# The scan's B and C rows: from selection matmuls to a store in memory and one broadcast transfer per state

## The chip, the cores and the metric

The kernel runs on one core of a Trainium2 chip. The metric is the device time of one execution in microseconds (us). The kernel before has a median of 2842.82 us over three runs (2838.62 to 2860.75).

## What is computed

The input is eight sequences (b = 0 to 7) of 512 tokens with 128 features. Each passes through a layer norm, a Mamba block with what follows it (norms, a gated attention-like step, a small MLP), a mixture of experts in which a sequence picks 2 of 8, then causal attention with 16 heads of width 64, then a second mixture of experts in which each token picks 2 of 8. The change touches the Mamba block alone, whose core is the recurrence

```python
x_dbl = u @ x_proj_w.T
dt, Bm, C = jnp.split(x_dbl, [DT_RANK, DT_RANK + D_STATE], axis=-1)
delta = jax.nn.softplus(dt @ dt_proj_w.T + dt_proj_b)
def step(h, t):
    delta_t, B_t, C_t, u_t = t
    dA = jnp.exp(delta_t[..., None] * A)
    h = dA * h + delta_t[..., None] * B_t[:, None, :] * u_t[..., None]
    y = jnp.einsum('bdn,bn->bd', h, C_t)
    return (h, y)
```

There are 16 states n and 256 inner channels. Everything is float32.

## The kernel before

Features or inner channels lie on the 128 partitions and the 512 tokens along the row, so the 256 inner channels are two halves, 1024 values in a row. For one state n the recurrence over time is one scan instruction on VectorE. It takes three VectorE instructions in `front_step` (lines 1239 to 1262): D1 = DU x B (line 1245), the scan HS (line 1250), HC = HS x C (line 1262). ScalarE makes the decay factors DA (line 979), and GpSimd adds HC into Y (line 1601). B and C of one state are one row of 512 numbers each, the same for all 128 partitions, and they are needed on all of them. A selection matmul makes this: PE multiplies a 96 x 128 matrix of ones and zeros (`pick`, line 1140) by S3, which holds the 32 rows of B and C three times as bfloat16 parts that add up to float32, and leaves the row on all partitions of a PSUM bank (FB for B, line 635; FC for C, line 642). The three parts are made by six VectorE instructions, lines 1200 to 1209.

The work goes in laps, one for a sequence (`laps`, line 437). A lap has phase 1, in which the rest of the Mamba block and the first experts of sequence b are interleaved with the second experts of b-1 and the beginning of the Mamba block of b+1 (`front_start`), and phase 2, the attention of b with the 16 scan steps of b+1 laid between (f is b+1). The first sequence's Mamba block stands alone ahead of the first lap (`front`); its 16 scan steps follow each other with nothing else to do. The last lap has no scan.

Phase 2 is 64 tiles n, a tile being 128 query rows of one head; eight tiles are a pair of heads (j is the pair, i = n % 8 the place in it). The order of each engine is written out by hand:

- PE per tile: transposes of the probabilities (`turn`, line 832), the scores of tile n+3 (lines 821, 824), the product with the values of tile n-1 (line 844). At i = 0 and 2 it also projects q and k of the next pair (line 812). At i = 0 and 4 it makes B of a state, at i = 1 and 5 C.
- VectorE per tile: the row maximum of tile n+2 (line 1484), at i = 0 and 2 the rotated product for the next pair (line 1478), at i = 1 the division of the last pair (line 1496); then at i = 1, 2, 3 the parts D1, scan, HC of one state, and at i = 5, 6, 7 those of the next.
- ScalarE: the exponentials (line 1063), the copies of the transposes (line 1071), the bias for the rotation (line 1051).
- GpSimd: per rotation two additions or products (lines 1615 and 1618) at i = 0 and i = 2, and the addition into Y at i = 3 and i = 7.
- SyncE issues all transfers from one queue. In phase 2 these are the swaps of neighbouring rows for the rotation (`swap_pairs`, lines 505 to 513), two of 64 x 512 for each.

The scores use a ring of three PSUM banks, so PE can be at most about three tiles ahead of the exponentials, and these wait for the maxima.

## Time and profile before

| | |
|---|---|
| median of three runs | 2842.82 us |
| the profiled execution | 2849.43 us |
| its span, first to last instruction | 2847.6 us |
| PE busy | 2609.8 us, 92% |
| VectorE busy | 1804.3 us, 63% |
| ScalarE busy | 1235.0 us, 43% |
| GpSimd busy | 754.6 us, 27% |
| mean granted TensorE clock | 0.929 |

Busy shares are over the whole span. In the timeline a row is one instruction, or several of one kind in a row (x2, x4); instructions of one engine overlap a little, since the next one starts while the last drains. "Idle before" is how long the engine stood still ahead of a row, and behind the arrow stands what ended it. A clock of 1.00 is TensorE's full 2.4 GHz, 0.50 is 1.2 GHz.

### The profile page before, as it was taken

To read this page: it belongs to the slowest core of one execution; us is meant where nothing else is said; L and a number is where in the kernel's file an instruction comes from. 1 tells how busy PE (TensorE), PEld (TensorE's weight loads), DVE (VectorE), ACT (ScalarE), POOL (GpSimd) and SP (SyncE) were. 2 spreads that over 40 slices of the span, in tenths; PEclk is the share of its full clock that TensorE was granted. 3 is DMA by queue.
4 is the path that set the end of the run, shared out by engine and by line. 5 is a ranking of instruction groups with operands and counts; after the bars stand their busy time and mean duration, and the time that the engine had idled before them with its cause. 6 is when DMAs were issued, how large, how long until landed. Compare 5 with 4: busy or idle time off the path is not lost.

```text
span 2847.6 us, 35881 instructions
## 1 busy us (share of the span) xinstructions
PE 2609.8 (92%) x10560; PEld 1426.0 (50%) x10560; DVE 1804.3 (63%) x3214; ACT 1235.0 (43%) x2672; POOL 754.6 (27%) x429
## 2 busy tenths in 40 slices
PE   3267999999999999999999999999989999999999
PEld 1033555445554455545555455544555455545654
DVE  3953786567765677657866587557765587644334
...
DMA packets 28590, 61.76 MB, mean 22 GB/s; under 512 B 5464, under 2 KB 5856, under 8 KB 27744
## 3 DMA queue, kind: packets, MB, share of 16 engines
...
## 4 chain that ended last, share of the span: by engine, by line
PE 76%; issue 10%; DVE 8%; ACT 3%; POOL 2%; DMA 0%; SPq 0%; DVEq 0%; POOLq 0%; ACTq 0%
PE G L844 10%; PE G L821 9%; PE G L768 6%; PE G L769 6%; PE G L778 5%; PE G L832 5%; PE FM L821 5%; PE G L812 2%; PE G L861 2%; DVE HS L1250 2%; PE FM L748 2%; PE FM L596 2%; PE G L824 2%; PE G L568 2%; PE FM L812 1%
## 5 line engine op out<-in xcount | busy, mean ns | idle before, releaser
L1032 ACT ACTIVATE HS<-G 128x512 f32<-128x512 f32 x256 | 152.6, 596 | 608.4 <-PE G L769 607.1
L1601 POOL TENSOR_TENSOR Y<-Y,HC 128x1024 f32<-128x1024 f32 x128 | 301.1, 2352 | 351.3 <-DVE HC L1262 351.3
L844 PE MATMUL G<-REG 128*128 128x64 f32 x2560 | 383.4, 283 | 1.8
L1615 POOL TENSOR_TENSOR REG<-REG,cos_t 128x512 f32<-128x512 f32 x128 | 219.8, 1717 | 621.8 <-ACT REG L1051 621.8
L1413 DVE SCALAR_TENSOR_TENSOR HS<-HS,G 128x512 f32<-128x512 f32 x256 | 175.8, 687 | 298.7 <-ACT HS L1032 296.1
L844 PEld LDWEIGHTS G<-REG 128*128 128x128 f32 x2560 | 346.2, 201 | 11.0 <-ACT REG L1071 5.6
L1071 ACT ACTIVATE REG<-G 128x128 f32<-128x128 f32 (+3 forms) x512 | 222.2, 434 | 219.1 <-PE G L832 213.2
L1250 DVE TENSOR_TENSOR_SCAN HS<-DA,D 128x1024 f32<-128x1024 f32 x128 | 312.8, 2444 | 1.3
L821 PE MATMUL G<-REG 64*128 64x256 f32 (+3 forms) x688 | 289.8, 503 | 11.5 <-ACT REG L1063 11.3
L768 PE MATMUL G<-D,up_w 128*128 128x512 f32 x512 | 270.7, 611 | 7.8 <-DVE HC L1420 7.0
L778 PE MATMUL G<-HC,down_w 128*128 128x512 f32 x512 | 265.0, 602 | 3.9 <-DVE HC L1420 3.9
L769 PE MATMUL G<-D,gate_w 128*128 128x512 f32 x512 | 266.8, 603 | 0.0
L832 PE MATMUL G<-ident,REG 128*128 128x128 f32 x1280 | 237.7, 285 | 3.4 <-ACT REG L1071 2.9
L1578 POOL COPY XNB<-XN 128x512 f32<-128x512 f32 x8 | 4.9, 610 | 882.2 <-DVE REG L1389 867.5
L1484 DVE TENSOR_REDUCE maxes<-G 128x1 f32<-128x128 f32 (+3 forms) x344 | 164.1, 478 | 102.4 <-PE G L824 102.4
L1063 ACT ACTIVATE REG<-G,maxes 128x128 f32<-128x128 f32 (+3 forms) x344 | 179.5, 522 | 104.6 <-DVE maxes L1484 100.3
L979 ACT ACTIVATE DA<-DELTA,a_neg 128x511 f32<-128x511 f32 x256 | 180.2, 710 | 63.1 <-DVE HS L1250 62.9
L1420 DVE SCALAR_TENSOR_TENSOR HC<-HS,G 128x512 f32<-128x512 f32 x256 | 176.0, 688 | 25.6
L821 PEld LDWEIGHTS G<-REG 64*128 64x128 f32 x688 | 106.6, 194 | 156.8 <-issue 88.8
L1618 POOL TENSOR_TENSOR REG<-REG 128x512 f32<-128x512 f32 x128 | 168.0, 1312 | 58.7 <-DMA REG<-ROT 52.0
L832 PEld LDWEIGHTS G<-ident,REG 128*128 128x128 f32 x1280 | 172.1, 169 | 5.7 <-issue 4.8
L821 PE MATMUL FM<-REG 64*128 64x128 f32 (+3 forms) x336 | 145.4, 514 | 21.0 <-ACT REG L1043 18.9
...
## 6 DMA issues: line engine op xcount, KB each, us to landing
REG<-ROT SPq DMA_DIRECT2D x256, 128.0 KB, 2.0
EW<-experts SPq DMA_DIRECT2D x16, 514.5 KB, 4.1
...
```

The source lines that it names most:

```text
L768: pe.matmul(G[g][:, :], up_w[:, e, c * P:(c + 1) * P], XS[:, e % 2, :], start=True, stop=True)
L769: pe.matmul(G[g + 1][:, :], gate_w[:, e, c * P:(c + 1) * P], XS[:, e % 2, :], start=True, stop=True).then_inc(ug_mm.sem, 1)
L778: pe.matmul(G[4][:, :], down_w[:, n // CHUNKS, n % CHUNKS, :], HH[:, n % 4, :], start=n == 0, stop=n == T_STEPS - 1, skip_group_check=True ...
L821: pe.matmul(bank[:, 0:width], QK[lo:lo + DK, j % 2, 0, t * P:(t + 1) * P], QK[lo:lo + DK, j % 2, 1, 0:width], start=True, stop=False)
L832: mm = pe.transpose(G[2][:, c * P:(c + 1) * P], PR[:, n % 2, c * P:(c + 1) * P], ident[:, :])
L844: mm = pe.matmul(G[3][:, col:col + DK], PT[:, n % 2, c * P:(c + 1) * P], V[:, c, j * P + h * DK:j * P + (h + 1) * DK], start=c == 0, stop= ...
L979: act.activation(DA[:, n % 2, h, 1:S], DELTA[:, h, 1:S], ACT.Exp, scale=a_neg[:, h, n:n + 1]).then_inc(da_exp.sem, 1)
L1063: act.activation(PR[:, n % 2, 0:width], ring_bank[("score", n)][:, 0:width], ACT.Exp, bias=maxes[:, j % 2, i:i + 1], accum_out=rows[:, j % ...
L1071: act.activation(PT[:, n % 2, 0:width], G[2][:, 0:width], ACT.Copy).then_inc(pt_copy.sem, 1)
L1250: dve.tensor_tensor_scan(HS[:, :, :].rearrange("p h s -> p (h s)"), DA[:, n % 2, :, :].rearrange("p h s -> p (h s)"), D1[:, :, :].rearrang ...
L1601: pool.tensor_tensor(Y[:, :, :], Y[:, :, :], HC[:, n % 2, :, :], ALU.add).then_inc(y_add.sem, 1)
L1615: pool.tensor_tensor(ROT, ROT, cos_t[:, :], ALU.mult).then_inc(rope_d.sem, 1)
```

## The change

B and C of a sequence now come out of one float32 PSUM bank with 32 rows, are copied by one VectorE instruction to rows 32 to 63 of FT (BC), and are stored to a buffer in device memory (`bc_rows`, 32 x 512 float32, 64 KB). For each state one transfer reads its two rows and writes them to all 128 partitions (BCS, two buffers; 512 KB written per state). D1 and HC multiply by BCS, in SBUF, where they multiplied by FB and FC, in PSUM. The selection matmuls, the `pick` matrix, its source and the three-part split are gone. The load of state n waits for HC of state n-2.

```diff
-        row_of_sb = sb("row_of_sb", [96, 2 * STATES])
-        pick = sb("pick", [96, 2 * STATES, P], BF16)
-        S3 = sb("S3", [96, S], BF16)
-        S3B = sb("S3B", [96, S], BF16)
+        BCS = sb("BCS", [P, 2, 2, S])
-        R1, DT = FT[0:96, :], FT[0:RANK, :]
+        BC, DT = FT[32:32 + 2 * STATES, :], FT[0:RANK, :]
+        bc_rows = nc.dram_tensor("bc_rows", (2 * STATES, S), F32).ap()
...
+                if f is not None:
+                    store_bc(f)
+                    load_bc(f, 0)
+                    load_bc(f, 1)
                 if t is not None:
                     sp.wait_ge(out_d.sem, out_d.at(t))
                     sp.dma_start(outT[t], OUT).then_inc(out_st.sem, 16)
+
+            def store_bc(b):
...
+                sp.wait_ge(bc_copy.sem, bc_copy.at(b))
+                sp.sem_inc(sp_passed, 1)
+                sp.dma_start(bc_rows, BC).then_inc(bc_out.sem, 16)
+
+            def load_bc(b, n):
+
+                if n == 0:
+                    sp.wait_ge(bc_out.sem, bc_out.at(b))
+                    sp.sem_inc(sp_passed, 1)
+                if n >= 2:
+                    sp.wait_ge(hc_mul.sem, hc_mul.at(b, n - 1))
+                else:
+                    sp.wait_ge(hc_mul.sem, hc_mul.at(b - 1))
+                sp.sem_inc(sp_passed, 1)
+                sp.dma_start(BCS[:, n % 2, :, :], bc_rows.rearrange("(k n) s -> n k s", n=STATES)[n].partition_broadcast(P)).then_inc(bc_in[n % 2].sem, 16)
...
             def phase_2(b, f):
-                for m in range(2 * PAIRS):
-                    swap_pairs(b, m)
+                swap_pairs(b, 0)
+                swap_pairs(b, 1)
+                for n in range(N_TILES):
+                    j, i = n // PER_PAIR, n % PER_PAIR
+                    if i in PROJECT_AT and j + 1 < PAIRS:
+                        swap_pairs(b, 2 * (j + 1) + PROJECT_AT.index(i))
+                    if f is not None and i % 4 == 3 and n // 4 + 2 < STATES:
+                        load_bc(f, n // 4 + 2)
...
-                        mm = pe.matmul(out[0:96, :], w("x_bc", h * 96, 96), US[:, h, :], start=h == 0, stop=h == 1)
+                        mm = pe.matmul(out[0:2 * STATES, :], w("x_bc", h * 2 * STATES, 2 * STATES), US[:, h, :], start=h == 0, stop=h == 1)
...
-                pe.matmul(FB[:, :], pick[:, n, :], S3[:, :], start=True, stop=True).then_inc(b_mm.sem, 1)
...
-                pe.matmul(FC[:, :], pick[:, STATES + n, :], S3[:, :], start=True, stop=True).then_inc(c_mm.sem, 1)
...
-                    if f is not None and i % 4 == 0:
-                        front_b(f, 2 * j + i // 4)
-                    if f is not None and i % 4 == 1:
-                        front_c(f, 2 * j + i // 4)
...
-                    dve.tensor_copy(S3[:, :], out[0:96, :]).then_inc(bc_split.sem, 1)
...
-                    dve.tensor_copy(S3[64:96, :], R1[64:96, :]).then_inc(bc_split.sem, 1)
+                    dve.tensor_copy(BC, out[0:2 * STATES, :]).then_inc(bc_copy.sem, 1)
...
-                    dve.wait_ge(b_mm.sem, b_mm.at(b, n + 1))
+                    dve.wait_ge(bc_in[n % 2].sem, bc_in[n % 2].at(b, n // 2 + 1))
...
-                    dve.tensor_tensor(D1[:, :, :], DU[:, :, :], FB[:, :].unsqueeze(1).to_broadcast([P, HALVES, S]), ALU.mult).then_inc(db_mul.sem, 1)
+                    dve.tensor_tensor(D1[:, :, :], DU[:, :, :], BCS[:, n % 2, 0, :].unsqueeze(1).to_broadcast([P, HALVES, S]), ALU.mult).then_inc(db_mul.sem, 1)
...
-                    dve.tensor_tensor(HC[:, n % 2, :, :], HS[:, :, :], FC[:, :].unsqueeze(1).to_broadcast([P, HALVES, S]), ALU.mult).then_inc(hc_mul.sem, 1)
+                    dve.tensor_tensor(HC[:, n % 2, :, :], HS[:, :, :], BCS[:, n % 2, 1, :].unsqueeze(1).to_broadcast([P, HALVES, S]), ALU.mult).then_inc(hc_mul.sem, 1)
```

PE, phase 2, a stretch of the second pair of heads, tiles i = 0 to 2, in the kernel before (L812 projects q or k, L821 and L824 are a score, L832 the transposes, L844 the product with the values):

```order
L832 MATMUL G<-ident,REG 128x128
L635 MATMUL FB<-S,pick 128x512
L812 MATMUL G<-XN,W 128x512
L821 MATMUL G<-REG 128x512
L824 MATMUL G<-causal_bf,ident_bf 128x128
L844 MATMUL G<-REG 128x64 x4
L832 MATMUL G<-ident,REG 128x128 x2
L642 MATMUL FC<-S,pick 128x512
L821 MATMUL FM<-REG 128x128
```

and in the changed kernel, whose lines are 16 further down there:

```order
L848 MATMUL G<-ident,REG 128x128
L828 MATMUL G<-XN,W 128x512
L837 MATMUL G<-REG 128x512
L840 MATMUL G<-causal_bf,ident_bf 128x128
L860 MATMUL G<-REG 128x64 x4
L848 MATMUL G<-ident,REG 128x128 x2
L837 MATMUL FM<-REG 128x128
```

The two selection matmuls of a state are gone and the rest has kept its order.

VectorE, phase 2, from the division of a pair to the HC of its first state, in the kernel before, with what each waits for:

```order
L1496 TENSOR_TENSOR REG<-G,rows 128x512 [waits rec_d,pv_mm,ot_mm]
L1484 TENSOR_REDUCE maxes<-FM 128x1 [waits sc_mm]
L1245 TENSOR_TENSOR D<-DU,FB 128x1024 [waits b_mm]
L1484 TENSOR_REDUCE maxes<-G 128x1 [waits sc_mm]
L1478 SCALAR_TENSOR_TENSOR ROT<-G,V_,sin_t 128x512 [waits pj_mm,swap_in]
L1250 SCALAR_TENSOR_TENSOR HS<-DA,D 128x1024 [waits da_exp,db_mul]
L1484 TENSOR_REDUCE maxes<-FM 128x1 [waits sc_mm]
L1262 TENSOR_TENSOR HC<-HS,FC 128x1024 [waits y_add,c_mm,scan_d]
```

and in the changed kernel:

```order
L1493 TENSOR_TENSOR REG<-G,rows 128x512 [waits rec_d,pv_mm,ot_mm]
L1481 TENSOR_REDUCE maxes<-FM 128x1 [waits sc_mm]
L1243 TENSOR_TENSOR D<-DU,BCS 128x1024 [waits bc_in0]
L1481 TENSOR_REDUCE maxes<-G 128x1 [waits sc_mm]
L1475 SCALAR_TENSOR_TENSOR ROT<-G,V_,sin_t 128x512 [waits pj_mm,swap_in]
L1248 SCALAR_TENSOR_TENSOR HS<-DA,D 128x1024 [waits da_exp,db_mul]
L1481 TENSOR_REDUCE maxes<-FM 128x1 [waits sc_mm]
L1259 TENSOR_TENSOR HC<-HS,BCS 128x1024 [waits y_add,scan_d]
```

The order is the same. D1 waits for a transfer where it waited for a matmul, and D1 and HC read both inputs from SBUF where one came from a PSUM bank.

SyncE, phase 2, the swaps of one pair and the loads behind them, in the changed kernel; before, only the L538 rows stood here (as L513):

```order
L538 DMA REG<-ROT 64x512 [waits rope_d,rot_d]
L538 DMA REG<-ROT 64x512
L538 DMA REG<-ROT 64x512 [waits rope_d,rot_d]
L538 DMA REG<-ROT 64x512
L528 DMA BCS<-bc_rows 128x2x512 [waits hc_mul] x2
```

Two loads of 512 KB now stand between the second swap of a pair and the first of the next, in the same queue.

## Rows read from the trace of the kernel before

**Rows 1.** The page: busy time and share of the span, by engine

```profile
PE 2609.8 (92%) x10560; PEld 1426.0 (50%) x10560; DVE 1804.3 (63%) x3214; ACT 1235.0 (43%) x2672; POOL 754.6 (27%) x429
```

**Rows 2.** Busy time by stretch: a phase 1, then a phase 2

```profile
443.00:600.00 157.00, 156.11 (x509) 80.38 (x510) 92.04 (x222) 44.61 (x71) 6.04 (x5) 0.98 0.03 9
600.00:770.00 170.00, 162.56 (x812) 94.90 (x810) 129.29 (x178) 110.06 (x265) 89.55 (x50) 0.95 0.08 29
```

**Rows 3.** Timeline of PE: start, duration, tiles i = 0 and 1

```profile
661.74 0.38 PE L635 MATMUL FB<-S,pick 96*128 96x512 bf16 x1
661.96 1.02 PE L812 MATMUL FM<-XN,W 128*128 128x512 f32 x2
...
665.16 0.38 PE L642 MATMUL FC<-S,pick 96*128 96x512 bf16 x1
665.47 0.49 PE L821 MATMUL G<-REG 64*128 64x128 f32 x2
```

**Rows 4.** Timeline of VectorE over one pair of heads

```profile
660.64 1.21 DVE L1262 TENSOR_TENSOR HC<-HS,FC 128x1024 f32<-128x1024 f32 x1
...
663.02 0.75 DVE L1478 SCALAR_TENSOR_TENSOR ROT<-FM,V_,sin_t 128x512 f32<-128x512 f32 x1 [0.71 <-PE FM L812]
...
665.29 0.69 DVE L1496 TENSOR_TENSOR REG<-G,rows 128x512 f32<-128x512 f32 x1 [1.40 <-PE G L844]
...
666.49 1.21 DVE L1245 TENSOR_TENSOR D<-DU,FB 128x1024 f32<-128x1024 f32 x1
...
668.48 2.28 DVE L1250 TENSOR_TENSOR_SCAN HS<-DA,D 128x1024 f32<-128x1024 f32 x1
...
670.99 1.21 DVE L1262 TENSOR_TENSOR HC<-HS,FC 128x1024 f32<-128x1024 f32 x1
...
684.55 1.21 DVE L1245 TENSOR_TENSOR D<-DU,FB 128x1024 f32<-128x1024 f32 x1
```

**Rows 5.** Timeline of GpSimd over the same pair

```profile
661.93 2.35 POOL L1601 TENSOR_TENSOR Y<-Y,HC 128x1024 f32<-128x1024 f32 x1 [4.42 <-DVE HC L1262]
664.57 1.27 POOL L1615 TENSOR_TENSOR REG<-REG,cos_t 128x512 f32<-128x512 f32 x1 [0.30 <-ACT REG L1051]
666.53 1.27 POOL L1618 TENSOR_TENSOR REG<-REG 128x512 f32<-128x512 f32 x1 [0.69 <-DMA REG<-ROT]
669.37 2.46 POOL L1615 TENSOR_TENSOR REG<-REG,cos_t 128x512 f32<-128x512 f32 x1 [1.56 <-ACT REG L1051]
```

**Rows 6.** Timeline of the front's scan steps, VectorE and GpSimd

```profile
62.09 2.29 DVE L1250 TENSOR_TENSOR_SCAN HS<-DA,D 128x1024 f32<-128x1024 f32 x1
...
71.44 1.22 DVE L1245 TENSOR_TENSOR D<-DU,FB 128x1024 f32<-128x1024 f32 x1
...
71.67 2.34 POOL L1601 TENSOR_TENSOR Y<-Y,HC 128x1024 f32<-128x1024 f32 x1 [3.55 <-DVE HC L1262]
72.69 3.47 DVE L1250 TENSOR_TENSOR_SCAN HS<-DA,D 128x1024 f32<-128x1024 f32 x1
...
77.33 1.21 DVE L1245 TENSOR_TENSOR D<-DU,FB 128x1024 f32<-128x1024 f32 x1
```

**Rows 7.** Timeline, head of a phase 2: a GpSimd and a VectorE instruction

```profile
607.69 2.04 POOL L1618 TENSOR_TENSOR REG<-REG 128x512 f32<-128x512 f32 x1 [0.17 <-POOL REG L1615]
...
609.19 1.62 DVE L1232 TENSOR_TENSOR HS<-HS,D 128x1024 f32<-128x1024 f32 x1
```

**Rows 8.** Timeline of VectorE in the front: `pick`, and the copy behind the split

```profile
11.84 2.28 DVE L1140 CAST pick<-row_of_sb 96x4096 bf16<-96x4096 f32 x1
...
47.75 0.68 DVE L1213 COPY FT<-FM 8x512 f32<-8x512 f32 x1
```

**Rows 9.** DMA issues: count, KB each, us from issue to landing

```profile
REG<-ROT SPq DMA_DIRECT2D x256, 128.0 KB, 2.0
EW<-experts SPq DMA_DIRECT2D x16, 514.5 KB, 4.1
```

**Rows 10.** Busy time by stretch: one of four at this clock in that lap

```profile
972.00:982.00 10.00, 10.00 (x31) 5.96 (x31) 4.92 (x6) 3.34 (x10) 2.34 (x1) 0.50 0.00 0
```

More of the change, by code:

```diff
@@ L65 @@
 WEIGHTS = {}
-for _name, _n in (("in_res", INNER), ("x_bc", HALVES * 96), ("x_dt", HALVES * RANK),
+for _name, _n in (("in_res", INNER), ("x_bc", HALVES * 2 * STATES), ("x_dt", HALVES * RANK),
                   ("out_proj", HALVES * D), ("q", D), ("k", D), ("proj", D), ("fl", D), ("d1", HID),
@@ L227, in build @@
         dt_copy = signal("dt_copy")
-        bc_split = signal("bc_split", 6)
+        bc_copy = signal("bc_copy")
+        bc_out = signal("bc_out", 1, 16)
+        bc_in = [signal(f"bc_in{k}", STATES // 2, 16) for k in range(2)]
         dp_mm = signal("dp_mm", 2)
@@ L235, in build @@
         skip_y = signal("skip_y", 2)
-        b_mm, c_mm = signal("b_mm", STATES), signal("c_mm", STATES)
         da_exp = signal("da_exp", 2 * STATES)
@@ L337, in build @@
         by_pool = [du_d, skip_y, y_add, y_gate, xnb_d, rope_d]
-        by_sp = [x_in, xb_in, *ew_in, out_st, idx_rd, swap_in]
+        by_sp = [x_in, xb_in, *ew_in, out_st, idx_rd, swap_in, bc_out, *bc_in]
         F_STEPS, T_STEPS = 29, EXPERTS * CHUNKS
@@ L503, in phase_1 @@
                     sp.dma_start(outT[t], OUT).then_inc(out_st.sem, 16)
+            def store_bc(b):
+                for k in range(2):
+                    sp.wait_ge(bc_in[k].sem, bc_in[k].at(b - 1))
+                    sp.sem_inc(sp_passed, 1)
[10 more added lines that the diff above has]
+                    sp.wait_ge(hc_mul.sem, hc_mul.at(b - 1))
+                sp.sem_inc(sp_passed, 1)
+                sp.dma_start(BCS[:, n % 2, :, :], bc_rows.rearrange("(k n) s -> n k s", n=STATES)[n].partition_broadcast(P)).then_inc(bc_in[n % 2].sem, 16)
             def swap_pairs(b, m):
@@ L524, in front @@
                     sp.dma_start(dst, src).then_inc(s_late, 16)
+                store_bc(b)
+                for n in range(STATES):
+                    load_bc(b, n)
             laps(sp, front, phase_1, phase_2)
@@ L535, in _ @@
             pe.wait_ge(s_const, n_loads)
-            pe.wait_ge(s_made, 13)
+            pe.wait_ge(s_made, 12)
             def bank(key, b, f):
@@ L546, in bank @@
                     else:
-                        pe.wait_ge(hc_mul.sem, hc_mul.at(s))
+                        pe.wait_ge(relu_d.sem, relu_d.at(s))
                 else:
@@ L625, in front_delta @@
                 pe.matmul(FC[:, :], dt_lhs[:, P:INNER], DT, start=True, stop=True).then_inc(dp_mm.sem, 1)
-            def front_b(b, n):
-                if n:
-                    pe.wait_ge(db_mul.sem, db_mul.at(b, n))
-                else:
-                    pe.wait_ge(bc_split.sem, bc_split.at(b))
-                    pe.wait_ge(relu_d.sem, relu_d.at(b, 1))
-                pe.matmul(FB[:, :], pick[:, n, :], S3[:, :], start=True, stop=True).then_inc(b_mm.sem, 1)
-            def front_c(b, n):
-                if n:
-                    pe.wait_ge(hc_mul.sem, hc_mul.at(b, n))
-                else:
-                    pe.wait_ge(relu_d.sem, relu_d.at(b))
-                pe.matmul(FC[:, :], pick[:, STATES + n, :], S3[:, :], start=True, stop=True).then_inc(c_mm.sem, 1)
             def filter_step(b, p, f):
@@ L913, in front @@
                 front_delta(b, None)
-                for n in range(STATES):
-                    front_b(b, n)
-                    front_c(b, n)
             def late():
                 pe.wait_ge(s_late, n_late)
-                pe.wait_ge(s_made, 15)
+                pe.wait_ge(s_made, 14)
             laps(pe, front, phase_1, phase_2, late)
@@ L932, in _ @@
             act.activation(a_neg[:, :, :], a_neg[:, :, :], ACT.Exp).then_inc(s_alog, 1)
-            act.wait_ge(s_made, 13)
+            act.wait_ge(s_made, 12)
             def square(n, b):
@@ L943, in front_start @@
                     act.wait_ge(dp_mm.sem, dp_mm.at(f - 1))
+                    act.wait_ge(bc_out.sem, bc_out.at(f - 1))
                     square(n1, f)
@@ L1139, in _ @@
             dve.tensor_copy(causal_bf[:, :], causal_f).then_inc(s_made, 1)
-            dve.tensor_copy(pick[:, :, :], row_of_sb[:, :].unsqueeze(2).to_broadcast([96, 2 * STATES, P])).then_inc(s_made, 1)
             dve.tensor_copy(wg_cols[:, :], vec("w_g").to_broadcast([P, P])).then_inc(s_made, 1)
@@ L1560, in late @@
                 dve.tensor_scalar(q_b, q_b, DK ** -0.5, None, ALU.mult).then_inc(s_made, 1)
-                dve.wait_ge(s_made, 15)
+                dve.wait_ge(s_made, 14)
             laps(dve, front, phase_1, phase_2, late)
```

28 lines of the change are left out of this document (8 added, 20 removed).

## The prediction

> **What bounds the kernel now.** I read the page first. PE is busy 92% of the span, VectorE 63%, GpSimd 27% [rows 1]. The stretches say the same of both phases: PE 156.1 of 157 us in a phase 1, 162.6 of 170 in a phase 2 [rows 2]. So a matmul taken out is worth its time, if nothing else then comes last. VectorE is busy 129.3 of 170 us in phase 2 [rows 2], and there the change works, so I read one pair of heads engine by engine. The pair repeats every 684.55 - 666.49 = 18.06 us [rows 4]. In it VectorE waits for PE before the rotation (0.71 us) and before the division (1.40 us) [rows 4]: PE sets the pace, with VectorE a little behind. The front is different: there is no other work, VectorE never stops, and one scan step takes 77.33 - 71.44 = 5.89 us [rows 6].
>
> In the front a scan takes 3.47 us where the first took 2.29 [rows 6]. The first had no GpSimd work beside it; the later one starts at 72.69, inside the GpSimd addition that runs from 71.67 to 74.01, and ends at 76.16, 2.15 us after it. It did nothing until GpSimd was done. In phase 2 the reverse is seen: a GpSimd product of 1.27 us takes 2.46 when it is issued inside a scan (668.48 to 670.76) [rows 4, 5]. And a plain product of two SBUF operands, L1232, takes 1.62 us instead of about 1.22 when GpSimd runs until 609.73, 1.08 us before its end [rows 7]. The D1 product, which starts at 71.44 with one operand in PSUM, keeps its 1.22 us although GpSimd starts at 71.67, and GpSimd keeps its 2.34 [rows 6]. So on this chip a VectorE instruction with both inputs in SBUF and a GpSimd instruction exclude each other, and one with a PSUM input does not take part.
>
> The Trainium skill says this as a rule (SBUF — State Buffer, "Who interferes with whom"): a VectorE instruction with two SBUF inputs contends with a GpSimd instruction that reads SBUF, and the one that comes second blocks fully; one with at most one SBUF input does not. By that rule, the trace agrees, and the change puts 256 more instructions under the lock.
>
> **The change part by part.**
>
> *Selection matmuls, removed.* Start to start they take 661.96 - 661.74 = 0.22 and 665.47 - 665.16 = 0.31 us [rows 3], so 0.27. Phase 2 of seven laps has 7 x 32 = 224: 60 us of PE, 1.1 per pair. The 32 in the front lie under the scans and give nothing. This is the most that the laps can gain.
>
> *`pick` and the split.* `pick` takes 2.2 us ahead of the first matmul, which waits for it [rows 8]: -2.2. In the front the split holds the bank before the matmul of DT by one instruction of 0.7 us more than one copy does [rows 8]: -0.7. In the laps the split is VectorE work under a PE that is full (92.0 of 157 us busy) [rows 2]: 0, at most -0.7 a lap.
>
> *D1 and HC read SBUF twice.* Alone they should still take 1.21 us; the scan's and L1232's unblocked lengths give no reason for more. The cost is the exclusion.
>
> Front: GpSimd's addition becomes ready at 71.67, inside D1 (71.44 to 72.66) [rows 6]. It now waits about 1.0 us, the scan waits for it as today, and everything behind moves. Less the 0.14 us that a blocked instruction gains at the hand-over (2.15 against 2.29) it is 0.85; if nothing is gained and the whole D1 counts, 1.22. I take 1.0 for 15 steps: +15 (bounds +13 and +18; 0 if there is no exclusion).
>
> A pair in phase 2: the instructions that exclude each other are two each of D1, scan and HC, 2 x (1.21 + 2.28 + 1.21) = 9.40 us [rows 4], and on GpSimd two additions into Y and four of the rotation, 2 x 2.35 + 4 x 1.27 = 9.78 us [rows 5] (the 2.46 there is a 1.27 and its wait). Together 19.2 us, against a pair of 18.06. Ten hand-overs at 0.14 make it 17.8; between D1, scan and HC VectorE has a maximum of 0.2 to 0.3 us in which GpSimd sometimes has nothing, some 0.5: 18.3. Without gain at the hand-overs it is 19.7. So the shared access, which nobody waited long for, becomes as full as PE was. Going through the pair by hand, the places are: the second rotation's product and its sum stand in line behind the scan and HC, the addition into Y behind them, and so D1 or the scan of the second state (i = 5, 6) waits 1 to 2 us; the first D1 meets the rotation's sum (both start at about 666.5 [rows 4, 5]) and costs 0.5. Behind each of these on VectorE is the next row maximum, for which the exponential, the transposes and the next score wait. PE alone would want 18.06 - 1.1 = 17.0. The bounds are therefore 17.0 and 19.7. I take 18.7, nearer to 18.3 because the hand-over gain stands in two rows, and above it because PE, with a ring of three banks, will not take uneven maxima without loss. There are 7 x 7 pairs with rotations in them: 49 x 0.64 = +31 (bounds -54 and +80).
>
> The last pair of a lap has no rotations; its shared work is 14.1 us, but its last HC comes later by what the pair before left over: 0. The first has the routing of the tokens on VectorE beside it and PE already waits for VectorE there; D1 now also meets a rotation: +1 a lap, +7.
>
> *Transfers.* 128 loads of 512 KB. The nearest row is the expert transfer, 514.5 KB in 4.1 us [rows 9]. A load is issued behind HC of state n-2. In the front it has a whole step of 5.9 us or more; in a pair about half a pair, 9 us. So 4.1 us hides: 0. If a broadcast is slower, it costs what exceeds 5.9 in the front. The second load of a pair goes out about 1.2 us before the first swap of the next, in the same queue; the swap (2.0 us [rows 9]) would land at about 4.1 + 0.8 = 4.9 us after HC, and the rotation's sum will need it then. Also 0, with nothing to spare. The store of 64 KB lies in phase 1 or, in the front, beside softplus. On PE a matmul no longer waits for D1 or HC; it had not waited in phase 2.
>
> *Sum.* 2849.4 + 15 - 2.9 + 31 + 7 = 2899.5 for the profiled execution. That lies 6.6 above the median of the runs, so 2893.
>
> **The rivals.**
>
> A. *PE keeps the pace* (faster). VectorE is busy only 63% and waits 2.1 us in a pair [rows 1, 4]; if the exclusion falls into these waits, the 60 us come out in full. 2849.4 - 60 - 2.9 - 6.6 = 2780 without any cost in the front, 2795 with it. Against it: the shared work is longer than the pair that PE alone would want, 17.8 against 17.0.
>
> B. *Packed without loss.* The pair takes 18.06 as before, what PE gives is what the exclusion takes. Left are the front and the first pairs: 2849.4 + 12 + 7 - 6.6 = 2862.
>
> C. *The swap behind the load.* If a broadcast lands not after 4.1 but 5.6 us, as 128 copies of one 2 KB row might, each first swap is 1.5 us late, and with it the rotation's sum, the next rotated product on VectorE and the scan. 49 x 1.5 = +73: 2966. It decides from the point where load and swap together exceed 4.9 us. For it: one queue. Against: the setup's transfers, broadcasts among them, landed without delay.
>
> D. *The clock.* After gaps on PE the granted clock falls to 0.50 and a stretch of 10 us then does the work of 5; one lap has four of them [rows 10]. They begin in the first pair, where the change adds waiting. If each lap gets one such lap's 20 us: +100, 2990. Gaps of under 1 us within a pair, as I expect, do not look like those that made it fall.
>
> **How the numbers follow.** The forecast (a pair between 18.2 and 19.7) 0.57, A 0.13, B 0.20, C and D 0.10. Time 2893. The range takes in B, nearly all between it and A, and C: 2812 to 2975. The forecast's own range is 2872 to 2940. A change of under 1%, 28 us, is about what a measurement of this kernel cannot tell from none; that is 2814 to 2871. B is inside, a little of A's partial forms too. Faster 0.14, same 0.24, slower 0.62.
>
> **What would show it.** In the front a step of about 6.9 us instead of 5.89, with D1 at 1.22 and GpSimd's addition or the scan stretched. In a pair of phase 2, D1 and HC no longer all at 1.21 but many at 1.5 to 3 us, GpSimd's products too, VectorE's busy time up by some 100 us or more, and its waits for PE gone; in their place PE waits for the exponentials and these for the maxima. The pair at 18.7. PE's busy share below 92%. D1 never waits for the BCS transfer except perhaps at the very first. If D1 and HC stay at 1.21 everywhere with GpSimd beside them, the reading of the exclusion is wrong and A holds. If the rotation's sum waits for its swap longer than the 0.69 us in rows 5, C is at work. If the clock in the stretches falls below 0.95 in phase 2, D.

## The result and the profile after

The changed kernel takes 3001.36 us, the median of four runs (2989.34 to 3012.66), against 2851.78 us (2838.62 to 2870.98) for the kernel before: a ratio of 1.052, 95% interval 1.043 to 1.060. It is slower by some 5%. The sign was predicted; the size was not: 3001 lies outside the range of 2812 to 2975. The profiled execution took 2992.3 us, span 2990.5, at a mean granted clock of 0.879 where it was 0.929. Some executions of a kernel take over 1.5% longer than its fastest, at a lower granted clock: every ratio here leaves them out, the medians don't.

The page of the kernel after (busy time, clock by slice, the chain of waits, groups, DMA issues):

```profile
PE 2685.0 (90%) x10304; PEld 1477.5 (49%) x10304; DVE 1918.6 (64%) x3173; ACT 1223.3 (41%) x2672; POOL 839.0 (28%) x429
...
PEclk8567788999899899988889777997899978898999
...
PE 52%; issue 22%; POOL 12%; DVE 9%; ACT 2%; DMA 1%; POOLq 0%; SPq 0%; DVEq 0%; ACTq 0%
...
L1598 POOL TENSOR_TENSOR Y<-Y,HC 128x1024 f32<-128x1024 f32 x128 | 348.1, 2719 | 373.2 <-DVE HC L1259 373.2
...
L1248 DVE TENSOR_TENSOR_SCAN HS<-DA,D 128x1024 f32<-128x1024 f32 x128 | 375.1, 2930 | 1.3
...
L1073 ACT ACTIVATE REG<-G,maxes 128x128 f32<-128x128 f32 (+3 forms) x344 | 179.7, 522 | 153.2 <-DVE maxes L1481 152.3
L1615 POOL TENSOR_TENSOR REG<-REG 128x512 f32<-128x512 f32 x128 | 208.9, 1632 | 98.5 <-DMA REG<-ROT 90.4
...
L1243 DVE TENSOR_TENSOR D<-DU,BCS 128x1024 f32<-128x1024 f32 x128 | 194.3, 1518 | 2.6 <-POOL DU L1589 2.6
...
BCS<-bc_rows SPq DMA_DIRECT2D x128, 512.0 KB, 4.8
REG<-ROT SPq DMA_DIRECT2D x256, 128.0 KB, 2.1
```

and the groups of the kernel before that answer to four of them (before, the scan is L1250, the additions L1601 and L1618, the exponential L1063):

```profile
L1601 POOL TENSOR_TENSOR Y<-Y,HC 128x1024 f32<-128x1024 f32 x128 | 301.1, 2352 | 351.3 <-DVE HC L1262 351.3
...
L1250 DVE TENSOR_TENSOR_SCAN HS<-DA,D 128x1024 f32<-128x1024 f32 x128 | 312.8, 2444 | 1.3
...
L1063 ACT ACTIVATE REG<-G,maxes 128x128 f32<-128x128 f32 (+3 forms) x344 | 179.5, 522 | 104.6 <-DVE maxes L1484 100.3
...
L1618 POOL TENSOR_TENSOR REG<-REG 128x512 f32<-128x512 f32 x128 | 168.0, 1312 | 58.7 <-DMA REG<-ROT 52.0
```

PE has 256 matmuls of 512 columns less (10304 instead of 10560) and is nevertheless busy for 75 us more than in [rows 1]. Fewer instructions and more busy time means slower ones. VectorE grew by 114 us (the scan's mean from 2.44 to 2.93 us), GpSimd by 84: time that one spent shut out by the other. Two waits grew by half or more: the rotation's sum for its swap (52.0 to 90.4), and the exponential for the row maximum (100.3 to 152.3).

Where the time went can be summed from the timeline of VectorE, which divides once per pair of heads: 8 divisions and so 7 intervals ("pairs" below) in each of the seven laps with a scan. Each row below is one profiled execution; the columns hold sums over the seven laps, then how many of the 49 pairs are over 21 us, how often the granted clock falls to 0.50 within them, and how many of their microseconds are spent at 0.50 (where no fall is counted, these follow a fall ahead of the first division of a lap). The seventh pair of a lap has no rotations and is shorter (13.1 us before), so the sum is less than 49 usual pairs. The kernels of the experiments are in it already.

| kernel | first division at | 49 pairs | between the laps' pairs | usual pair | over 21 us | falls of the clock | us at 0.50 |
|---|---|---|---|---|---|---|---|
| before | 318.3 | 854.2 | 1454.2 | 18.06 | 1 | 0 | 23 |
| after | 329.2 | 979.0 | 1461.3 | about 19 | 14 | 19 | 260 |
| neither exclusion nor loads | 318.1 | 821.5 | 1428.7 | 17.47 | 0 | 0 | 11 |
| loads alone | 313.8 | 873.2 | 1432.7 | 18.0 | 3 | 4 | 76 |
| exclusion alone | 329.7 | 864.5 | 1467.2 | 18.18 | 1 | 0 | 36 |
| exclusion of HC alone | 318.0 | 829.0 | 1452.0 | 17.47 | 0 | 1 | 30 |
| exclusion of D1 alone | 333.0 | 845.0 | 1456.2 | 17.76 | 0 | 2 | 29 |
| loads behind swaps | 325.3 | 884.1 | 1455.8 | 18.55 | 0 | 5 | 49 |
| three buffers | 328.9 | 857.0 | 1455.5 | 18.18 | 0 | 1 | 20 |
| after, filled | 330.5 | 905.6 | 1466.8 | 19.1 | 1 | 0 | 18 |
| exclusion alone, filled | 331.3 | 881.2 | 1453.8 | 18.77 | 1 | 0 | 5 |
| B copied to PSUM | 315.2 | 823.7 | 1449.5 | 17.47 | 0 | 0 | 17 |
| B and C copied to PSUM (the second run) | 315.7 | 830.0 | 1439.0 | 17.64 | 0 | 0 | 14 |

Of the 142.9 us that the span grew, 10.9 lie ahead of the first division and 124.8 in the 49 pairs. In these the clock fell 19 times, and before the change never.

Ahead of it the front's step shows the exclusion as predicted. Timeline of VectorE and of GpSimd, kernel after:

```profile
61.39 1.22 DVE L1243 TENSOR_TENSOR D<-DU,BCS 128x1024 f32<-128x1024 f32 x1
62.64 4.31 DVE L1248 TENSOR_TENSOR_SCAN HS<-DA,D 128x1024 f32<-128x1024 f32 x1
66.98 1.22 DVE L1259 TENSOR_TENSOR HC<-HS,BCS 128x1024 f32<-128x1024 f32 x1
68.13 1.22 DVE L1243 TENSOR_TENSOR D<-DU,BCS 128x1024 f32<-128x1024 f32 x1
```

```profile
61.62 3.19 POOL L1598 TENSOR_TENSOR Y<-Y,HC 128x1024 f32<-128x1024 f32 x1 [5.06 <-DVE HC L1259]
```

GpSimd's addition starts inside D1 and now takes 3.19 us instead of 2.34 [rows 6]: it does nothing until D1 has ended, finishes at 64.81, and the scan, which was 3.47, is 4.31 and ends 2.14 us after it. The step is 68.13 - 61.39 = 6.74 us, 0.85 more than the 5.89 of [rows 6].

In a pair of phase 2 three engines are to be read together. Timeline of VectorE, GpSimd, SyncE and PE (only PE's rows with a wait), kernel after, lap 3. The SyncE rows are issues merged, and their length ends with the last issue, not with a landing:

```profile
1041.69 1.65 DVE L1243 TENSOR_TENSOR D<-DU,BCS 128x1024 f32<-128x1024 f32 x1
...
1044.25 0.75 DVE L1475 SCALAR_TENSOR_TENSOR ROT<-FM,V_,sin_t 128x512 f32<-128x512 f32 x1 [0.71 <-DMA REG<-ROT]
1044.92 2.71 DVE L1248 TENSOR_TENSOR_SCAN HS<-DA,D 128x1024 f32<-128x1024 f32 x1
...
1047.86 1.90 DVE L1259 TENSOR_TENSOR HC<-HS,BCS 128x1024 f32<-128x1024 f32 x1
...
1052.67 3.66 DVE L1248 TENSOR_TENSOR_SCAN HS<-DA,D 128x1024 f32<-128x1024 f32 x1
...
1056.57 1.21 DVE L1259 TENSOR_TENSOR HC<-HS,BCS 128x1024 f32<-128x1024 f32 x1
...
1060.88 1.64 DVE L1243 TENSOR_TENSOR D<-DU,BCS 128x1024 f32<-128x1024 f32 x1
```

```profile
1040.98 1.27 POOL L1612 TENSOR_TENSOR REG<-REG,cos_t 128x512 f32<-128x512 f32 x1
1044.20 1.27 POOL L1615 TENSOR_TENSOR REG<-REG 128x512 f32<-128x512 f32 x1 [1.95 <-DMA REG<-ROT]
1046.35 2.33 POOL L1612 TENSOR_TENSOR REG<-REG,cos_t 128x512 f32<-128x512 f32 x1 [0.88 <-ACT REG L1061]
1048.84 2.05 POOL L1615 TENSOR_TENSOR REG<-REG 128x512 f32<-128x512 f32 x1 [0.16 <-POOL REG L1612]
1050.85 3.34 POOL L1598 TENSOR_TENSOR Y<-Y,HC 128x1024 f32<-128x1024 f32 x1
```

```profile
1049.86 8.38 SPq L528 DMA_DIRECT2D BCS<-bc_rows  x2
1059.00 6.76 SPq L538 DMA_DIRECT2D REG<-ROT  x4
```

```profile
1041.32 0.41 PE L860 MATMUL G<-REG 128*128 128x64 f32 x2 [0.23 <-ACT REG L1081]
1044.08 0.66 PE L869 MATMUL G<-ident,REG 128*128 128x128 f32 x4 [0.37 <-ACT REG L1073]
1046.33 0.91 PE L837 MATMUL FM<-REG 64*128 64x384 f32 x2 [0.75 <-ACT REG L1061]
1048.59 1.12 PE L837 MATMUL G<-REG 64*128 64x512 f32 x2 [0.41 <-ACT REG L1073]
```

The pair is 1060.88 - 1041.69 = 19.19 us. The rotation's sum waits 1.95 us for its swap where it waited 0.69 [rows 5], and VectorE itself stands 0.71 us for that DMA. From D1's start to the scan's it is 3.23 us; before it was 668.48 - 666.49 = 1.99 [rows 4]. The last HC of the pair ends at 1057.78; the sum of the next pair waits until 1063.16, 5.4 us later (before: 4.7, from 661.85 to 666.53 [rows 4, 5]). PE, which was busy 162.6 of 170 us in a phase 2 [rows 2], waits in four small pieces of 0.23 to 0.75 us, 1.76 in all, for ScalarE, which waits for the maxima and for the rotation. In this pair the granted clock stays at 1.00.

### The profile page after: what moved, and what is told of

Its sections match the earlier page's. It is cut to its first block, busy times and chain, and to the rows that moved or that the text cites. A ratio compares the mean times of both kernels' runs of the same rounds, so it can differ in the third digit from the quotient of the medians.

```text
span 2990.5 us, 35609 instructions
## 1 busy us (share of the span) xinstructions
PE 2685.0 (90%) x10304; PEld 1477.5 (49%) x10304; DVE 1918.6 (64%) x3173; ACT 1223.3 (41%) x2672; POOL 839.0 (28%) x429
## 3 DMA queue, kind: packets, MB, share of 16 engines
q8 instruction: 97, 1.59, 0.2%
## 4 chain that ended last, share of the span: by engine, by line
PE 52%; issue 22%; POOL 12%; DVE 9%; ACT 2%; DMA 1%; POOLq 0%; SPq 0%; DVEq 0%; ACTq 0%
PE G L784 6%; PE G L785 6%; PE G L794 5%; PE G L860 5%; POOL REG L1615 4%; POOL REG L1612 4%; PE G L837 4%; DVE HS L1248 3%; POOL Y L1598 3%; PE FM L837 2%; PE G L848 2%; PE FM L764 2%; PE FM L630 2%; PE G L877 2%; PE G L602 2%
## 5 line engine op out<-in xcount | busy, mean ns | idle before, releaser
L1598 POOL TENSOR_TENSOR Y<-Y,HC 128x1024 f32<-128x1024 f32 x128 | 348.1, 2719 | 373.2 <-DVE HC L1259 373.2
L860 PE MATMUL G<-REG 128*128 128x64 f32 x2560 | 428.8, 306 | 9.4 <-ACT REG L1081 5.0
L860 PEld LDWEIGHTS G<-REG 128*128 128x128 f32 x2560 | 389.5, 223 | 20.5 <-issue 11.3
L1248 DVE TENSOR_TENSOR_SCAN HS<-DA,D 128x1024 f32<-128x1024 f32 x128 | 375.1, 2930 | 1.3
L837 PE MATMUL G<-REG 64*128 64x256 f32 (+3 forms) x688 | 320.6, 551 | 28.8 <-ACT REG L1073 14.8
L848 PE MATMUL G<-ident,REG 128*128 128x128 f32 x1280 | 262.5, 309 | 3.4 <-ACT REG L1081 2.7
L1073 ACT ACTIVATE REG<-G,maxes 128x128 f32<-128x128 f32 (+3 forms) x344 | 179.7, 522 | 153.2 <-DVE maxes L1481 152.3
L1615 POOL TENSOR_TENSOR REG<-REG 128x512 f32<-128x512 f32 x128 | 208.9, 1632 | 98.5 <-DMA REG<-ROT 90.4
L1243 DVE TENSOR_TENSOR D<-DU,BCS 128x1024 f32<-128x1024 f32 x128 | 194.3, 1518 | 2.6 <-POOL DU L1589 2.6
L848 PEld LDWEIGHTS G<-ident,REG 128*128 128x128 f32 x1280 | 192.2, 186 | 5.8 <-issue 3.8
L837 PE MATMUL FM<-REG 64*128 64x128 f32 (+3 forms) x336 | 163.2, 571 | 34.0 <-ACT REG L1053 19.6
## 6 DMA issues: line engine op xcount, KB each, us to landing
BCS<-bc_rows SPq DMA_DIRECT2D x128, 512.0 KB, 4.8
EW<-experts SPq DMA_DIRECT2D x16, 514.5 KB, 3.8
gate_w<-moe_gate SPq DMA_DIRECT2D x1, 2048.0 KB, 18.7
```

Of the source, the lines that this page charges most:

```text
L837: pe.matmul(bank[:, 0:width], QK[lo:lo + DK, j % 2, 0, t * P:(t + 1) * P], QK[lo:lo + DK, j % 2, 1, 0:width], start=True, stop=False)
L848: mm = pe.transpose(G[2][:, c * P:(c + 1) * P], PR[:, n % 2, c * P:(c + 1) * P], ident[:, :])
L860: mm = pe.matmul(G[3][:, col:col + DK], PT[:, n % 2, c * P:(c + 1) * P], V[:, c, j * P + h * DK:j * P + (h + 1) * DK], start=c == 0, stop= ...
L1243: dve.tensor_tensor(D1[:, :, :], DU[:, :, :], BCS[:, n % 2, 0, :].unsqueeze(1).to_broadcast([P, HALVES, S]), ALU.mult).then_inc(db_mul.sem, 1)
L1248: dve.tensor_tensor_scan(HS[:, :, :].rearrange("p h s -> p (h s)"), DA[:, n % 2, :, :].rearrange("p h s -> p (h s)"), D1[:, :, :].rearrang ...
L1598: pool.tensor_tensor(Y[:, :, :], Y[:, :, :], HC[:, n % 2, :, :], ALU.add).then_inc(y_add.sem, 1)
```

## The experiments

All edits are to the changed kernel unless another is named. Ratios are to the kernel before, run beside them, with 95% intervals. Where a kernel leaves work out, the text on record or the sentence ahead says so.

### The parts apart: neither, loads alone, exclusion alone

Without store and loads and the waits that belong to them, D1 and HC reading two PSUM banks that nothing writes for them (the result is then not the scan's):

```diff
-    store_bc(f)
-    load_bc(f, 0)
-    load_bc(f, 1)
...
-    dve.tensor_tensor(D1[:, :, :], DU[:, :, :], BCS[:, n % 2, 0, :]...
+    dve.tensor_tensor(D1[:, :, :], DU[:, :, :], FB[:, :]...
-    dve.tensor_tensor(HC[:, n % 2, :, :], HS[:, :, :], BCS[:, n % 2, 1, :]...
+    dve.tensor_tensor(HC[:, n % 2, :, :], HS[:, :, :], FC[:, :]...
```

> The changed kernel without its store and loads, and with D1 and HC reading the old PSUM banks FB and FC, which hold what the step before left there (no B or C is selected or loaded, so the scan computes with other numbers). It is what is left when the selection matmuls alone are taken out. All theories: PE sets the pace, a pair of heads takes 17.2 us against 18.06, and the time is about 60 us under the kernel before, 2785 to 2800, with the granted clock as before (0.93).

Measured: 2796.52 us, ratio 0.987 (0.983 to 0.991). The time is the expected one, the pair is not: 17.47 us instead of 17.2. The next keeps store and loads, whose data nobody reads, with D1 and HC on PSUM as above.

> As x1, but with the store and the 128 loads of 512 KB, whose data nobody reads (D1 and HC read the old PSUM banks). Theory T (the exclusion of VectorE and GpSimd makes the loss): within 10 us of x1. Theory Q (the swap of the rotation stands behind a load in the one queue, and what waits for it makes the loss): 30 us or more above x1, GpSimd's wait for the swap from 0.7 to 2 us a pair, pairs of 18 us or more.

Measured: 2842.57 us, ratio 0.999 (0.995 to 1.003), most pairs 17.9 to 18.2 and three over 21, as Theory Q had it. Its group of the rotation's sum:

```profile
L1615 POOL TENSOR_TENSOR REG<-REG 128x512 f32<-128x512 f32 x128 | 168.0, 1312 | 107.6 <-DMA REG<-ROT 98.0 <-POOL REG L1612 7.2 <-PE G L840 1.9
```

The sum itself is back at its 1312 ns, and the wait for the swap is 98.0 us, with no exclusion at all; without the loads it is 53.7. The loads make the swap late by themselves.

The third has D1 and HC on SBUF, as in the change, but no store and no loads; BCS holds a constant:

```diff
-    store_bc(f)
-    load_bc(f, 0)
-    load_bc(f, 1)
...
+    dve.memset(BCS[:, :, :, :], 0.01)
...
-    dve.wait_ge(bc_in[n % 2].sem, bc_in[n % 2].at(b, n // 2 + 1))
```

> The changed kernel without its store and loads: D1 and HC read both inputs from SBUF, BCS being filled once with a constant (B and C are not the computed ones). Theory T: most of the loss is here, 100 us or more above x1, D1, scan and HC stretched as in the changed kernel, and PE's gaps with a lower granted clock. Theory Q: within 30 us of x1. If the two act together, x3 lies between: a pair of 18.3 at full clock, 40 to 60 us above x1.

Measured: 2877.12 us, ratio 1.013 (1.007 to 1.020), pair 18.18. Timeline of VectorE, one pair:

```profile
1727.45 1.65 DVE L1233 TENSOR_TENSOR D<-DU,BCS 128x1024 f32<-128x1024 f32 x1
...
1729.88 2.49 DVE L1238 TENSOR_TENSOR_SCAN HS<-DA,D 128x1024 f32<-128x1024 f32 x1
...
1732.61 1.90 DVE L1249 TENSOR_TENSOR HC<-HS,BCS 128x1024 f32<-128x1024 f32 x1
```

The same blocked D1 and HC as in the full change, but the scan starts 2.43 us after D1 instead of 3.23. So of the 1.24 us by which that distance grew, the exclusion made 0.44 and the loads beside it 0.80. With the loads alone it is usually 2.1 us, hardly more than before: the late swap holds up the scan by that much only where the exclusion is there too. The time lies between the theories, but 81 us above x1 where 40 to 60 were expected.

What follows from the three: the removed matmuls and the split are worth 42 us (2838.77 against 2796.52), and by the medians the loads add 46 to that, the exclusion 81. The ratios are the better scale, since the changed kernel itself was measured at another time, beside other runs of the kernel before: 0.9991 - 0.9868 = 1.2 points for the loads and 1.0133 - 0.9868 = 2.65 for the exclusion, together a ratio of 1.026. The changed kernel is at 1.052. The 2.6 points between, some 74 us and well beyond the intervals, belong to neither alone.

### The loads moved: behind the swaps, and into a third buffer

```diff
-    if f is not None and i % 4 == 3 and n // 4 + 2 < STATES:
+    if f is not None and i == 3 and n // 4 + 2 < STATES:
         load_bc(f, n // 4 + 2)
+    if f is not None and i == 2 and j:
+        load_bc(f, 2 * j + 1)
```

> The changed kernel with the load of every second state issued behind the second swap of the next pair instead of ahead of the first. Nothing else changed. Theory T: within 20 us of the changed kernel. Theory Q: 50 us or more faster, the rotated product's wait for the swap gone.

Measured: 2891.56 us, ratio 1.020 (1.015 to 1.026), pair 18.55. The wait for the swap fell from 90.4 us to 34.0, but D1 now waits 50.7 us in total for its load, which it never did in the changed kernel. A wait was exchanged for a smaller one. The time is Theory Q's (3.1 points of ratio less than the changed kernel); the wait shrank and isn't gone.

With three buffers both loads of a pair can go out in the middle of it, ahead of any need. (Three counters that no engine waits for are also made one, here and in the versions that copy to PSUM.)

```diff
-    BCS = sb("BCS", [P, 2, 2, S])
+    BCS = sb("BCS", [P, 3, 2, S])
...
-    if f is not None and i % 4 == 3 and n // 4 + 2 < STATES:
-        load_bc(f, n // 4 + 2)
+    if f is not None and i == 3:
+        for k in (2 * j + 2, 2 * j + 3):
+            if 3 <= k < STATES:
+                load_bc(f, k)
```

> The changed kernel with three buffers for B and C instead of two and both loads of a pair issued in tile i = 3, so that no load is near a swap and each is issued a whole pair or half of one ahead of D1. If the queue is the whole difference between the changed kernel and the one without loads: 2865 to 2890, as x3 (2877), pairs of 18.2, no wait of D1 for BCS. If transfers cost something that is not their place in the queue: 2900 or more.

Measured: 2879.46 us, ratio 1.014 (1.007 to 1.022); usual pair 18.18, wait for the swap 38.4 us, no D1 waiting. That is the time, the pair and (38.5) the swap's wait of the exclusion alone, as the first of the two expectations has it, although all 128 loads of 512 KB are made, at 4.9 us each. The loads cost nothing by their bytes; what they cost is where they stand in the queue. Merely moving them takes 3.6% off the changed kernel.

### The clock: filler matmuls

One matmul of 512 bfloat16 columns per tile of phase 2, 448 in all, into a bank that nothing uses:

```diff
+    if f is not None:
+        if n == 0:
+            pe.wait_ge(relu_d.sem, relu_d.at(f))
+        pe.matmul(FB[:, :], ident_bf[:, :], FILL[:, :], start=True, stop=True)
```

> The changed kernel with one more bfloat16 matmul of 512 columns behind the transposes of every tile of phase 2 while there is a scan; its result is not read. 448 matmuls of some 0.22 us are 99 us more work for PE, 1.8 us a pair. Theory C (the gaps that exclusion and queue leave on PE make the clock fall, and the pairs at half clock are half of the loss): the fillers stand in PE's gaps, the granted clock rises from 0.88 to 0.92 or more, pairs of 22 to 27 us become rare, and the time is not above that of the changed kernel and may be 50 us under it. Theory N (the clock is no cause; PE's waits for maxima are): the time rises by 30 to 99 us and the clock stays.

Measured: 2919.17 us, ratio 1.027 (1.019 to 1.035): PE has more to do and the kernel is 82 us faster than the changed one by the medians, some 70 by the ratios (1.052 against 1.027). Stretches of phase 2 in lap 2, first the kernel after and then the filled one (busy time of PE, PEld, DVE, ACT, POOL; then the granted clock, DMA share, GB/s):

```profile
700.00:710.00 10.00, 8.19 (x35) 4.48 (x34) 8.15 (x9) 5.61 (x15) 6.57 (x5) 0.81 0.30 88
710.00:720.00 10.00, 10.00 (x48) 5.65 (x47) 7.81 (x8) 5.34 (x15) 3.81 (x2) 0.85 0.27 62
...
740.00:750.00 10.00, 8.65 (x41) 5.22 (x40) 9.27 (x9) 5.96 (x15) 7.20 (x5) 0.85 0.25 89
750.00:760.00 10.00, 10.00 (x44) 5.47 (x42) 7.51 (x8) 5.11 (x15) 3.52 (x2) 0.80 0.22 65
```

```profile
700.00:710.00 10.00, 9.99 (x57) 6.22 (x57) 8.34 (x10) 5.82 (x16) 5.34 (x3) 1.00 0.34 99
710.00:720.00 10.00, 9.70 (x54) 5.55 (x52) 8.94 (x11) 6.32 (x18) 7.98 (x4) 1.00 0.26 73
...
740.00:750.00 10.00, 9.99 (x55) 5.90 (x55) 8.38 (x12) 5.91 (x15) 4.49 (x4) 1.00 0.27 80
750.00:760.00 10.00, 9.81 (x60) 6.05 (x57) 9.29 (x8) 6.16 (x16) 8.09 (x4) 1.00 0.24 79
```

Read the first fence in pairs of rows: a stretch in which PE has gaps (8.19 and 8.65 of 10 us busy), in or behind which the granted clock leaves 1.00, and then one in which PE is busy throughout and yet does only 48 or 44 matmuls, where the filled kernel, fillers included, does 54 to 60. Some of the time PE runs there at the lower of its two levels, 1.2 instead of 2.4 GHz. With the fillers the clock is 1.00 in all these rows, it doesn't fall once within the 49 pairs, and of the 14 pairs over 21 us one is left. That is Theory C. The waits that make the gaps are still there: the rotation's sum still waits 90.2 us for its swap.

What PE did ahead of the fall in 740:750, kernel after (only its rows with a wait; the granted clock is 1.00 until 747 and 0.54 in the microsecond behind it):

```profile
739.48 0.41 PE L860 MATMUL G<-REG 128*128 128x64 f32 x2 [0.23 <-ACT REG L1081]
742.23 0.66 PE L869 MATMUL FM<-ident,REG 128*128 128x128 f32 x4 [0.37 <-ACT REG L1073]
744.30 0.91 PE L837 MATMUL G<-REG 64*128 64x384 f32 x2 [0.58 <-ACT REG L1061]
746.56 1.59 PE L837 MATMUL G<-REG 64*128 64x512 f32 x2 [0.41 <-ACT REG L1073]
```

Four waits, 1.59 us in all, and none is longer than 0.58. Shortly ahead of each of the 19 falls PE had waited at least twice; in 13 of them no single wait was over 0.88 us, in the other six one was 1.0 to 2.3. But the pair of lap 3 above has the same four waits with 1.76 us in all, and its clock stays at 1.00. What decides between the two is not shown.

The trace gives the clock's price without the fillers too. In the kernel after, lap 3 has 6.8 us at half clock in its seven pairs and they take 128.4 us; lap 5 has 62.0, and they take 149.9. That is 21.5 us for 55.2 at half clock, 0.39 each. The 49 pairs have 260 - 23 = 237 us more at half clock than before: an estimate of 92 us.

To see whether fillers gain anywhere, the same were put into the version with the exclusion alone.

> The control for the filled version of the changed kernel: the same 448 filler matmuls (their result is never used) in the version without loads, where D1 and HC read a constant from SBUF and so compute wrong numbers at the right cost. Without fillers this version took 2877.12 us with pairs of 18.18 us and hardly any of 22 to 27 us. Theory (the fillers gain only by keeping the clock up where the loads had let it fall): there is little to win here and up to 99 us of TensorE's work to pay, part of it inside its gaps; 2865 to 2925 us, not below 2865. Rival (fillers gain in any version, by some other way than the gaps that the loads make): the same gain as in the changed kernel, about 80 us, so 2795 to 2830 us.

Measured: 2895.96 us, ratio 1.017 (1.013 to 1.022), pair 18.77 instead of 18.18. Here they cost: 0.59 us a pair, 16.7 us in the 49 pairs, and 19 us by the medians (0.4 points by the ratios, whose intervals overlap). The gain of 80 us that the rival wanted is excluded. So of these two versions the fillers gain in the one whose clock falls. The two filled versions also give what the loads cost when the clock stays up: 905.6 - 881.2 = 24 us in the 49 pairs.

### The exclusion: D1 or HC

The version with the exclusion alone, with D1 on PSUM and so HC's exclusion only:

```diff
-    dve.tensor_tensor(D1[:, :, :], DU[:, :, :], BCS[:, n % 2, 0, :]...
+    dve.tensor_tensor(D1[:, :, :], DU[:, :, :], FB[:, :]...
```

> As x3 (no loads, a constant in BCS), but D1 reads the old PSUM bank FB, so only HC and the scan read both inputs from SBUF. Half of the exclusion. In the front the step should be 5.9 us as in the kernel before, since only D1 met the addition there. In a pair HC still meets the rotation, and the first and second D1 no longer hold up anything: between x1 (2796) and x3 (2877), nearer to x1, 2805 to 2840, a pair of 17.5 to 17.9.

Measured: 2818.29 us, ratio 0.993 (0.990 to 0.996); pair 17.47, front step 5.9, both as with no exclusion; the ratio is 0.6 points higher than there, with intervals that just overlap. In the other, HC reads FC in PSUM and D1 reads BCS. (The text on record has the two letters exchanged: D1 reads B from SBUF, and HC reads its C from a bank that nothing writes.)

> This kernel is the changed one without its loads (BCS holds a constant), with D1's exclusion alone: D1 reads C from SBUF, and HC reads B from a PSUM tile that nothing writes; both products are wrong numbers at the right cost. Theory (all of the exclusion's price is D1, HC's costs nothing): the pair is 18.2 us, as with both, the time 2860 to 2885 us, and the time of a half-tile step in the opening stage 6.74 us. Rival (the two share the price, and HC's came for free only where D1's was gone): the pair is 17.7 to 18.0 us and the time 2835 to 2860 us.

Measured: 2835.04 us, ratio 0.998 (0.994 to 1.003); pair 17.76, front step 6.74. This was the rival's pair, and the time stands at the edge of its range. Alone, HC's exclusion costs no pair time, and D1's 0.29 us; together they cost 0.71. In the front D1 makes all of it, since it is D1 that delays GpSimd's addition. In a pair HC is blocked just as long without D1's exclusion, but nothing comes of it. One pair with HC's exclusion alone, VectorE and GpSimd:

```profile
1706.19 1.91 DVE L1249 TENSOR_TENSOR HC<-HS,BCS 128x1024 f32<-128x1024 f32 x1
...
1709.09 1.20 DVE L1233 TENSOR_TENSOR D<-DU,FB 128x1024 f32<-128x1024 f32 x1
...
1711.01 2.68 DVE L1238 TENSOR_TENSOR_SCAN HS<-DA,D 128x1024 f32<-128x1024 f32 x1
```

```profile
1709.19 2.36 POOL L1588 TENSOR_TENSOR Y<-Y,HC 128x1024 f32<-128x1024 f32 x1
```

and the same scan and addition of a pair with both exclusions:

```profile
1737.42 3.66 DVE L1238 TENSOR_TENSOR_SCAN HS<-DA,D 128x1024 f32<-128x1024 f32 x1
```

```profile
1735.60 3.33 POOL L1588 TENSOR_TENSOR Y<-Y,HC 128x1024 f32<-128x1024 f32 x1
```

HC takes 1.91 us alone and 1.90 with both. What differs comes behind it: GpSimd's addition starts beside the second D1. With D1 on PSUM it runs at once (2.36 us) and the scan behind takes 2.68; with D1 on SBUF it has to wait for D1 (3.33), and the scan for it (3.66). It is the meeting of the two that costs.

By the ratios HC's share on top of D1's is 1.5 points, 43 us, give or take some 22 by the two intervals. The two profiled executions differ by 2885.2 - 2857.8 = 27.4 us, of which 19.5 are in the pairs (864.5 - 845.0) and 11.0 between the laps' pairs. So no stage hides the rest: the profiled execution of the version with D1 alone was 24.5 us above its median (2859.57 against 2835.04), that of the other 9.8.

### Versions that compute everything

If an operand in PSUM takes VectorE out of the exclusion, the rows can be loaded as in the change and then be copied to PSUM by ScalarE, which is busy 41%. Loads go out at i = 3 and 6, and D1 and HC read the copies:

```diff
+    act.activation(FB[:, :], BCS[:, n % 2, 0, :], ACT.Copy).then_inc(b_cp.sem, 1)
...
+    act.activation(FC[:, :], BCS[:, n % 2, 1, :], ACT.Copy).then_inc(c_cp.sem, 1)
```

> A version that keeps the transfers and removes both costs: ScalarE copies B and C of each state from BCS into the PSUM banks FB and FC (256 copies of 512 values, about 0.6 us each, 2.4 us a pair), D1 and HC read PSUM as in the kernel before, and the loads are issued in tiles i = 3 and i = 6, away from the swaps. It computes everything. If exclusion and queue are the only costs, it keeps PE's gain: 2795 to 2815, a pair of 17.3 to 17.6, faster than both kernels. If ScalarE's 2.4 us delay the exponentials: 2830 to 2870.

Measured: 2806.73 us, ratio 0.990 (0.982 to 0.998), pair 17.64: the time of the first expectation, the pair just above its 17.3 to 17.6. In five rounds once more:

> The complete version with both of B and C copied to PSUM by ScalarE once more, in five rounds beside the other, to settle its ratio. Theory: 2800 to 2820 us, a ratio of 0.985 to 0.993 to the kernel before, pair 17.6 us. Rival (the first ratio was luck): a ratio of 0.995 to 1.005.

Measured: 2811.27 us, ratio 0.988 (0.984 to 0.993). That is the theory's range, and it beats both kernels. And with three buffers, only B copied (the first line above) and HC reading C from SBUF:

> A complete version that computes everything. B and C come by broadcast loads issued at tile 3 of a pair into one of three SBUF buffers; ScalarE copies only C's counterpart B... that is, B's rows, into PSUM, and D1 reads what ScalarE copied while HC reads SBUF directly. Theory (HC's exclusion is free, D1's costs, and the spread loads no longer delay the swap): pair 17.5 us, as in the run with neither exclusion nor loads, time 2795 to 2815 us. Rival (each of ScalarE's copies delays an exponential that TensorE's sums wait for, or loads still cost bandwidth): pair 17.8 to 18.2 us, time 2830 to 2880 us.

Measured: 2816.7 us, ratio 0.991 (0.989 to 0.994), pair 17.47, exactly that of the version with neither exclusion nor loads; the time is 2 us above the theory's range. Halving the copies gains 0.17 us a pair, but the total isn't better: the intervals of the two overlap. Both are about 1% faster than the kernel before.

## Why the prediction was wrong, step by step

- **The exclusion: right in mechanism, right in size in the front, too large in a pair.** The front's step grew by 0.85 us, which is the lower value named (2.15 against 2.29 at the hand-over); 1.0 was taken. The pair added up came to 18.3 and measures 18.18 with the exclusion alone; 18.7 was taken. So the +31 us of the sum is 864.5 - 854.2 = +10 there, removed matmuls included. HC and D1 are stretched as foretold (1.90, 1.65), and the exponentials wait for the maxima. The Trainium skill's rule (SBUF — State Buffer, "Who interferes with whom") is borne out both ways: 17.47 us with HC and D1 on PSUM, 18.18 with both on SBUF.
- **The removed matmuls: mis-sized.** The pair was put at 17.0 without them; it is 17.47. They and the split gave 42 us by the medians instead of 63. A matmul taken out of an engine that is 96% busy was not worth all of its time.
- **The transfers at "0, with nothing to spare": failed.** The prediction said the swap "would land at about 4.1 + 0.8 = 4.9 us after HC, and the rotation's sum will need it then". The broadcast takes 4.8 us and not 4.1, and the sum was served 5.4 us after HC. It also wanted the swap earlier than assumed: by [rows 5] it was already waiting for the last 0.69 of its 4.7 us, so it wanted it after 4.0. No cover was left before the change, and any further delay made that wait longer. That is rival C's mechanism, at 24 / 49 = 0.5 us a pair with the clock up (the filled versions), not 1.5. The test named for it, a wait above 0.69, came true at 1.95.
- **The clock: dismissed, and most of the error.** Rival D was set aside with "Gaps of under 1 us within a pair, as I expect, do not look like those that made it fall", and was looked for in the first pair of a lap. It came in the middle of phase 2, and in 13 of 19 falls behind waits of which none was over 0.88 us. Each cause alone leaves the clock up in nearly all pairs (1 over 21 us with the exclusion, 3 with the loads; 0 and 4 falls), both together have 14 and 19 falls. D was also priced carelessly: 20 us in each of seven laps are 140, where +100 was taken, and its 2990 was left outside the range that took in C. Its time comes near the measured one, but the place was another.
- **The sum, corrected.** Of the 124.8 us in the 49 pairs, the matmuls make 821.5 - 854.2 = -33, the exclusion 864.5 - 821.5 = +43, the loads beside it at full clock +24. The remaining 90 is what falls away with the fillers (979.0 - 905.6 = 73, and the 17 that they cost themselves); the estimate from the time at half clock is 92. So it is the clock. With the front's 11 this is nearly what the span shows. The steps that failed are therefore the clock, put at nothing and worth some 90 us, and the transfers, put at 0 and worth 24.
- **What was luck.** Without the clock the forecast would have been near: after and filled, the kernel takes 2919. But that is two errors against each other. The 49 pairs would have grown by -33 + 43 + 24 = 34 us against the +31 of the sum, because a pair taken too long made room for transfers taken at nothing.

A page of the Trainium skill (TensorE: Matmul & The Clock Gate, "A second HAM failure mode: psum-queue depth-cycling") describes PE idling in tiny pieces between groups of matmuls so often that the clock oscillates; there it is the cycling through PSUM banks that makes the pieces, here the waits for ScalarE. The runs agree that small pieces do it, with waits of 0.23 to 0.58 us ahead of the fall shown. It was the rule to weigh against this change.
